# Row maxima of the first attention head computed among the z projections

## The reference

```
qkv    = xn @ qkvw + qkvb                     # 32 heads of 32 features
scores = q k^T / sqrt(32); probs = softmax(scores); ctx = probs v
attn   = ctx @ ow + ob
gate   = softmax over the top 16 of 64 router scores (0 elsewhere)
z      = xn @ A_w^T                            # 64 experts x rank 8 = 512 columns
ffn    = (z * gate) @ B_w^T * 2
out    = x + attn + ffn
```

## Time and profile before

| | us |
|---|---|
| median of 3 runs | 2616.61 |
| profiled execution | 2617.83 |
| its span, first to last instruction | 2615.8 |
| TensorE (PE) busy | 2553.2 |
| GpSimd (POOL) busy | 1603.8 |
| VectorE (DVE) busy | 1511.7 |
| ScalarE (ACT) busy | 1216.7 |

### The profile page before, as it was taken

The page is one execution under the profiler, slowest core; times in us unless marked ns, Lnnn a source line. Parts: engine busy times, 40 slices in busy tenths (PEclk is TensorE's granted clock), DMA queues, the critical chain, the costliest instruction groups (busy, mean ns, idle before and its releaser), DMA issues. The chain is left out here.

```text
span 2615.8 us, 34875 instructions
## 1 busy us (share of the span) xinstructions
PE 2553.2 (98%) x13032; PEld 1655.5 (63%) x13032; DVE 1511.7 (58%) x2522; ACT 1216.7 (47%) x2299; POOL 1603.8 (61%) x529
## 2 busy tenths in 40 slices
PE   7999999999989999999999999999999999969999
PEld 6788888777745555555555555555555555428887
DVE  8511111111188888887888887888878888522231
ACT  2211111111006666666666666666666666650000
POOL 0110011110009999999999999999999999942111
PEclk9999999999959999999999999999999999989999
DMA  4233334121256778778787787787787787523332
GB/s 153 89 121 120 120 117 133 56 72 64 87 143 123 152 159 167 148 162 166 146 166 158 154 166 152 155 170 151 157 169 150 159 167 152 120 97 107 112 113 95
DMA packets 168168, 351.01 MB, mean 134 GB/s; under 512 B 89632, under 2 KB 114720, under 8 KB 137376
## 3 DMA queue, kind: packets, MB, share of 16 engines
q0 software_dynamic: 22320, 162.54, 32.2%
q1 hardware_dynamic: 145712, 186.70, 25.0%
HBM read 122.44 MB, written 63.69 MB: 71 GB/s over the span
## 5 line engine op out<-in xcount | busy, mean ns | idle before, releaser
L921 DVE TENSOR_REDUCE part_max<-ps_b 128x1 f32<-128x512 f32 x2048 | 1252.6, 681 | 276.1 <-PE ps_b L800 276.0
L747 POOL TENSOR_TENSOR psum_p<-psum_p,probs 128x2048 f32<-128x2048 f32 x254 | 1183.6, 4660 | 51.5 <-ACT probs L907 40.1
L907 ACT ACTIVATE probs<-ps_b 128x512 f32<-128x512 f32 x1924 | 971.7, 623 | 350.1 <-PE ps_b L789 348.0
L800 PE MATMUL ps_b<-kp,qp 96*128 96x512 f32 x2048 | 831.4, 413 | 14.5 <-DMA qp<-qk_scr 14.3
L789 PE MATMUL ps_b<-qp,kp 97*128 97x512 f32 x2048 | 840.1, 413 | 5.2 <-ACT probs L907 5.1
L789 PEld LDWEIGHTS ps_b<-qp,kp 97*128 97x128 f32 x2048 | 384.7, 189 | 348.1 <-issue 208.2
L816 PE MATMUL ps_b<-probs,vh 128*32 128x512 f32 x3848 | 468.4, 600 | 0.0
L800 PEld LDWEIGHTS ps_b<-kp,qp 96*128 96x128 f32 x2048 | 397.5, 194 | 101.4 <-DVE part_max L921 38.7
L236 POOL TENSOR_TENSOR wlo<-wraw,whi 128x1024 fp32r<-128x1024 f32 x29 | 69.4, 2395 | 613.2 <-ACT whi L339 613.2
L265 PE MATMUL ps_a<-xhi,whi 128*128 128x512 f32 (+1 forms) x928 | 370.7, 399 | 1.1 <-DVE elo L428 0.9
L265 PE MATMUL ps_a<-xlo,whi 128*128 128x512 f32 (+1 forms) x928 | 367.6, 396 | 0.0
(11 more groups left out here) (79 smaller groups left out, 1159.8 us busy)
## 6 DMA issues: line engine op xcount, KB each, us to landing
psum_q<-probs POOLq DMA_DIRECT2D x155, 1024.0 KB, 7.7
kp<-qk_scr SPq DMA_DIRECT2D x96, 256.0 KB, 4.1
qp<-qk_scr SPq DMA_DIRECT2D x96, 256.0 KB, 7.9
qk_scr<-ehi SPq DMA_DIRECT2D x16, 1024.0 KB, 3.9
qk_scr<-elo SPq DMA_DIRECT2D x16, 1024.0 KB, 6.7
wraw<-wcat SPq DMA_DIRECT2D x29, 512.5 KB, 7.5
craw<-cz_scr SPq DMA_DIRECT2D x16, 768.0 KB, 5.0
stage<-x SPq DMA_DIRECT2D x16, 512.0 KB, 3.8
```

Source lines behind the costliest of these rows:

```text
L747: pool.tensor_tensor(acc[:, :], first[:, :], tile(h, t)[:, :], ALU.add).then_inc(pool_done, 1)
L800: pe.matmul(ps[:, ring_bank(u), :], qp[s][0:PACK, tn * P:(tn + 1) * P], kp[s][0:PACK, b * NQ:(b + 1) * NQ], start=True, stop=True).then_in ...
L907: act.activation(tile(h, t)[:, b * NQ:(b + 1) * NQ], ps[:, n % ST_BANKS, :], ACT.Exp, scale=SCALE).then_inc(exp_done, 1)
L921: dve.tensor_reduce(part_max[hn % 2][:, tn, b:b + 1], ps[:, ring_bank(u), :], AX_X, ALU.max) \
```

## The change

- The space of `ehi` is allocated outside the stages and shared with a new tile `qk0`, which holds `qp` and `kp` of slot 0. `part_max0` too lives through both stages.
- **In stage a**, once all v transposes have been read, SyncE loads q and k of head 0 into `qk0` (six DMAs), and GpSimd sets row 96 of its keys to 1. From the third quarter of the z blocks on, five maxima tiles of head 0 are put among the 24 matmuls of each quarter (after k = 0, 2, 3, 5, 6), four in the last but one, none in the last: 64 in all. They use banks 4 to 7 in turn. VectorE reduces them before it reads that quarter's z product. After the last z matmul TensorE transposes the row maxima, VectorE negates them, and SyncE writes them into row 96, behind the last z stores, and waits for that.
- **In stage b** the prelude is gone. Head 0 starts with `scores_t` at once. The 80 maxima that had to be there by the end of head 0 (64 of head 1, 16 of head 2) are laid among its steps: none in step 0, six a step in steps 1 to 5, five a step in steps 6 to 15. From head 1 on, the order is as before. TensorE no longer waits for identity and ones at the start, but at the first transpose and at head 1. SyncE loads k and q of head 1, then v of heads 0 and 1, then k, q and v of head 2, then `w_early`.
- **In stage c** `xt` and `res` lie in the space of `ehi`.

```diff
@@ stage a, SyncE, ahead of the z stores
+            for u in range(2):
+                sp.wait_ge(stored[u], 32 * QK_BLOCKS // 2)
+            sp.wait_ge(vtr_ready, QB * V_BLOCKS)
+            for row, dst in ((0, qp0), (D, kp0)):
+                for r, hl in enumerate((0, 0, 1) if row == 0 else (0, 1, 0)):
+                    sp.dma_start(dst[r * HD:(r + 1) * HD, :].bitcast(F32), qk_scr[hl, row:row + HD, :]) \
+                        .then_inc(kq0_loaded, 16)
@@ stage a, SyncE, behind the z stores
+            sp.wait_ge(neg0_ready, 1)
+            sp.dma_start(qp0[PACK:PACK + 1, :].bitcast(F32), neg_max0[:, :]).then_inc(negmax0_loaded, 16)
+            sp.wait_ge(negmax0_loaded, 16)
@@ stage a, TensorE
+        def maxima0(q):
+            return [divmod(n, QB) for n in range(5 * (q - 2), min(5 * (q - 1), QB * TT))] if q >= 2 else []
+        def bank0(t, b):
+            return 4 + (QB * t + b) % 4
...
-            for b in range(Z_BLOCKS):
-                qk_block(b % 2, Z0 + b)
+            def maximum0(t, b):
+                n = QB * t + b
+                if n == 0:
+                    pe.wait_ge(kq0_loaded, 16 * 6)
+                    pe.wait_ge(lo_done, quarter(Z0 - 1, 3))
+                wait(pe, max0_free, n - 3)
+                pe.matmul(ps[:, bank0(t, b), :], qp0[0:PACK, t * P:(t + 1) * P], kp0[0:PACK, b * NQ:(b + 1) * NQ],
+                          start=True, stop=True).then_inc(max0_ready, 1)
+            for z in range(Z_BLOCKS):
+                blk = Z0 + z
+                pe.wait_ge(wlo_done, blk + 1)
+                for nb in range(QB):
+                    pe.wait_ge(lo_done, quarter(blk - 1, nb))
+                    left0 = maxima0(QB * z + nb)
+                    n = 0
+                    for k in range(KT):
+                        wk, tk = slice(k * P, (k + 1) * P), slice(nb * NQ, (nb + 1) * NQ)
+                        for w, xx in ((whi, xhi), (whi, xlo), (wlo, xhi)):
+                            last = pe.matmul(ps[:, nb, :], w[:, (z + 1) % 2, wk], xx[:, k, tk],
+                                             start=(n == 0), stop=(n == 3 * KT - 1))
+                            n += 1
+                        if left0 and k in (0, 2, 3, 5, 6):
+                            maximum0(*left0.pop(0))
+                    last.then_inc(mm_ready, 1)
+            pe.wait_ge(rowmax0_ready, 1)
+            pe.wait_ge(max0_free, QB * TT)
+            pe.transpose(ps[0:TT, 4, 0:P], row_max0[:, :], ident[:, :]).then_inc(flip0_ready, 1)
@@ stage a, VectorE, in the z blocks
+                    for t, n in maxima0(QB * b + nb):
+                        dve.wait_ge(max0_ready, QB * t + n + 1)
+                        dve.tensor_reduce(part_max0[:, t, n:n + 1], ps[:, bank0(t, n), :], AX_X, ALU.max) \
+                            .then_inc(max0_free, 1)
@@ stage b, the order of the maxima
-        def first_step(h):
-            return 0 if h >= 0 else -LEAD
+        def maxima_at(h, t):
+            if h == 0:
+                first, count = (6 * (t - 1), 6) if t < 6 else (30 + 5 * (t - 6), 5)
+                return [(1 + n // 64, n // QB % TT, n % QB) for n in range(first, first + count)] if t else []
+            hn, tn = (h + 1, t + LEAD) if t + LEAD < TT else (h + 2, t + LEAD - TT)
+            return [(hn, tn, b) for b in range(QB)] if hn < HEADS else []
@@ stage b, SyncE
-            for h in range(SLOTS):
-                load_keys(h)
-                load_queries(h)
-                load_values(h)
+            load_keys(1)
+            load_queries(1)
+            load_values(0)
+            load_values(1)
+            load_keys(2)
+            load_queries(2)
+            load_values(2)
...
-            load_negmax(0)
@@ stage b, TensorE
-            pe.wait_ge(ident_done, 2)
-            pe.wait_ge(ones_done, 1 + SLOTS)
...
             def step(h, t):
+                ahead = maxima_at(h, t)
                 for b in range(QB):
-                    if h >= 0:
-                        scores_t(h, t, b)
-                    if has_maxima(h, t):
-                        scores(h, t, b)
+                    scores_t(h, t, b)
+                    for u in ahead[b:b + 1]:
+                        scores(*u)
+                for u in ahead[QB:]:
+                    scores(*u)
```

More of the change, by code:

```diff
@@ L242, in _ @@
                     split(blk, (u + 1) % 2)
+            pool.wait_ge(wlo_done, BLOCKS)
+            pool.wait_ge(vtr_ready, QB * V_BLOCKS)
+            pool.memset(kp0[PACK:PACK + 1, :].bitcast(F32), 1.0).then_inc(ones0_done, 1)
+            pool.wait_ge(ones0_done, 1)
         @block.tensor
@@ L525, in sem @@
             return ctx.enter_context(nc.semaphore(name))
[L527 to L528 removed]
+        kp = [qk0[:, 1, :]] + [sb(f"kp{s}", [P, T], F32R) for s in range(1, SLOTS)]
+        qp = [qk0[:, 0, :]] + [sb(f"qp{s}", [P, T], F32R) for s in range(1, SLOTS)]
         vh = [sb(f"vh{s}", [P, TT, HD]) for s in range(SLOTS)]
@@ L538, in attend @@
         recip_b = sb("recip_b", [P, NQ])
-        part_max = [sb(f"part_max{s}", [P, TT, QB]) for s in range(2)]
+        part_max = [part_max0, sb("part_max1", [P, TT, QB])]
         row_max = [sb(f"row_max{s}", [P, TT]) for s in range(2)]
@@ L571, in attend, with loads @@
         ctx_stored = [sem("ctx_stored0"), sem("ctx_stored1")]
[L574 to L579, removed]
-        def first_step(h):
-            return 0 if h >= 0 else -LEAD
+        def loads(h):
+            return h // SLOTS + (1 if h % SLOTS else 0)
+        def maxima_at(h, t):
[4 more added lines that the diff above has]
+            return [(hn, tn, b) for b in range(QB)] if hn < HEADS else []
         ring_order = []
-        for h in range(-1, HEADS):
-            for t in range(first_step(h), TT):
-                if has_maxima(h, t):
-                    ring_order += [("max", h, t, b) for b in range(QB)]
+        for h in range(HEADS):
+            for t in range(TT):
+                ring_order += [("max", *u) for u in maxima_at(h, t)]
                 if t == SUMS_AT and h >= 1:
@@ L731, in _ @@
             pool.memset(ones[:, :], 1.0).then_inc(ones_done, 1)
-            for s in range(SLOTS):
-                pool.wait_ge(ones_done, s + 1)
+            for s in range(1, SLOTS):
+                pool.wait_ge(ones_done, s)
                 pool.memset(kp[s][PACK:PACK + 1, :].bitcast(F32), 1.0).then_inc(ones_done, 1)
-            pool.wait_ge(ones_done, SLOTS + 1)
+            pool.wait_ge(ones_done, SLOTS)
             def add(h, t):
@@ L790, in scores_t, with scores @@
                           qp[s][0:PACK + 1, b * NQ:(b + 1) * NQ], start=True, stop=True).then_inc(st_ready, 1)
-            def scores(h, t, b):
-                hn, tn = target(h, t)
+            def scores(hn, tn, b):
                 s = hn % SLOTS
-                u = ("max", h, t, b)
+                u = ("max", hn, tn, b)
                 wait_ring(pe, u)
                 if tn == 0 and b == 0:
-                    pe.wait_ge(kq_loaded[s], 16 * 6 * (hn // SLOTS + 1))
+                    pe.wait_ge(kq_loaded[s], 16 * 6 * loads(hn))
                 pe.matmul(ps[:, ring_bank(u), :], qp[s][0:PACK, tn * P:(tn + 1) * P],
@@ L861, in step @@
                     sums(h - 1)
[L863 to L866, removed]
+            for h in range(HEADS):
+                if h >= 1:
+                    pe.wait_ge(ones_done, SLOTS)
+                    pe.wait_ge(negmax_loaded[h % SLOTS], 16 * loads(h))
+                for t in range(TT):
                     step(h, t)
@@ L941, in row_maxima @@
             def row_maxima(h):
-                dve.wait_ge(mx_free, 64 * (h + 1))
+                dve.wait_ge(mx_free, 64 * h)
                 dve.tensor_reduce(row_max[h % 2][:, :], part_max[h % 2][:, :, :], AX_X, ALU.max) \
                     .then_inc(rowmax_ready, 1)
[L946 to L950, removed]
+            for h in range(HEADS):
+                for t in range(TT):
+                    for u in maxima_at(h, t):
+                        take_max(*u)
                     if t == RECIPROCAL_AT and h >= 1:
                         reciprocal(h - 1)
-                    if target(h, t)[1] == TT - 1 and h < LAST:
+                    if (h + 1, TT - 1, QB - 1) in maxima_at(h, t):
                         row_maxima(h + 1)
@@ L981, in project_output @@
         clo = sb("clo", [P, 2, OUT_KT, P], F32R)
-        xt = sb("xt", [P, 2, D])
+        xt, res = (ehi[:, i, :].rearrange("p (u d) -> p u d", u=2) for i in range(2))
         ob = sb("ob", [P, D])
-        res = sb("res", [P, 2, D])
         ps = ctx.enter_context(nc.psum_tensor("ps_c", [P, 8, NQ], F32))
```

67 lines of the change are left out of this document (42 added, 25 removed).

## The result

| | before | after |
|---|---|---|
| median | 2616.45 us (4 runs, 2615.69 to 2617.17) | 2596.57 us (4 runs, 2594.53 to 2597.29) |
| profiled execution | 2617.83 us | 2596.82 us |
| its span | 2615.8 us | 2595.0 us |

The ratio after to before is 0.9922, 95% interval 0.9907 to 0.9938: 19.9 us faster. The forecast was 24.6 us faster, 2592.0 us; the time lies 4.6 us above it and inside the range of 2586 to 2603.

What follows compares the result with a forecast made beforehand. VectorE and latencies were taken to bound the prelude, TensorE the steady heads. Terms 14.9 + 0.3 + 5.2 + 0.3 + 9.1 + 53.4 + 0.3 = 83.5 us against 108.1 gave 2592.0 us, range 2586 to 2603.

Steps and rivals of the forecast that it cites:

- The bound named: Prelude bound by VectorE reductions and latencies, steady heads by TensorE; the change attacks only the former stretch, 108.1 us before.
- Maxima among the z products: Stage a, z blocks: 64 added matmuls cost TensorE 14.9 us, with nothing extra for changing operand height.
- Rival C: Z blocks: changes of operand height cost 0.1 us each, 12.8 us more, giving 2605 us; chance 0.08.
- Six loads in front: Stage a: head 0's q and k loads land about when TensorE wants them; 0.3 us, bounds 0 and 3.
- End of stage a: Gap after the last z matmul: the negated maxima are written beside the stores; 0.3 us on top of 5.2.
- Start of head 0: Stage b's start: TensorE stands 9.1 us until the loads of head 1 land, as before the change.
- Its cover: Start of stage b: v of head 0, ones, identity, ScalarE's preparation and `w_early` stay hidden; GpSimd starts earlier, not later.
- Steps 1 to 15: Head 0: VectorE's 80 reductions, coupled to TensorE by four banks, plus low clock take 53.4 us; bounds 47.6 and 56.
- The idling at each pair: Head 0: VectorE idles 0.86 us at each of seven pairs of `values`, 6.0 us in all.
- D: Head 0: the ring couples less, TensorE's own 47.6 us for steps 1 to 15, giving 2586 us; chance 0.10.
- Rivals A and B: Head 0's clock swings, +17 us, 2609 us, chance 0.06; or stays low throughout, +35 us, 2627 us, chance 0.04.
- E: Nothing moves, since loads, block start or something else fills the freed time: 2616 us; chance 0.02.

Runs made afterwards that it cites:

- the changed kernel's second profile: The changed kernel timed again without edits, as reference for the follow-up runs: median 2596.38 us; its profiled z blocks last 110.5 us.
- idle matmuls: Changed kernel plus 24 matmuls with unused result ahead of TensorE's wait for the loads of head 1: median 2596.77 us.
- `values` in each step: Changed kernel with head 0's values one tile in each step instead of two in every second step: median 2595.58 us.
- loads-first kernel: Changed kernel with head 0's six q and k loads issued before the last v block's stores and next weight load: median 2593.83 us.

## Why the prediction was right, and where it was off

- **The bound named.** The prelude went, the rest of the heads did not move, and head 0, from its first maximum on, took 54.0 us, against the whole head's 46.4 before, because of VectorE. Right.
- **Maxima among the z products, 14.9 us.** Measured without the stand: 104.4 us to the transpose, against 716.50 + 0.23 - 627.05 = 89.7 to the same point before: 14.7. Rival C is out: operands of 96 and 128 rows alternate at 0.233 us.
- **Six loads in front, 0.3 us of 0 to 3.** This is the step that was mis-sized. The stand was 2.9, the end of the range, and I gave it no clock: behind it the matmuls ran at 1.2 GHz and cost 1.5 more. For a queue that held 1.5 MB of stores and weights I took the 9.1 us of an empty one. Together 4.4 us for 0.3, and 110.5 - 104.4 = 6.1 in the changed kernel's second profile, so this term alone went past its bound of 3.
- **End of stage a.** The write of the negated maxima did go beside the stores: the gap is 5.3 us, before 5.2.
- **Start of head 0.** 9.3 us as carried over. Its cover held: no wait of TensorE for v of head 0 or for the ones is in the trace there. GpSimd began head 0 at 757.83 us, 47.1 before head 1, where 46 were forecast.
- **Steps 1 to 15.** 54.0 for 53.7. The idling at each pair is 0.72, not 0.86, and the early pairs 7.98, not 8.06; the low clock lasted 4.5 us from the first maximum, 750.94 to 755.4, and cost 1.1 by the idle matmuls, not 0.7. Seven pairs at 0.14 less and a clock dearer by 0.4 would give 53.1; the 0.9 us up to the 54.0 seen are not accounted for, and that the sum came out 0.3 off is in part luck. D is out, since VectorE binds.
- **Rivals A and B, the clock.** It did fall to 1.2 GHz twice and rose again: once behind the stand in z, and once in the gap between the stages, where TensorE stood 5.2 us, from where it stayed low to 755.4. From 755.5 to 805 it is 1.00, through all of the full rings; TensorE's waits for a bank there are 0.4 us at most. So the swing that the Trainium skill's "TensorE: Matmul & The Clock Gate" describes under "A second HAM failure mode: psum-queue depth-cycling" did not come in head 0. It is not ruled out for other pauses of this kernel: in head 30, with waits of 0.30 us, the clock dips in some profiled executions and not in others.
- **E** is out: 19.9 us are gained.

## What to carry to other kernels

A load moved into the shadow of other work is priced with what stands in its queue at that place, and a stand inside dense matmuls with the slow clock behind it: here 2.9 us became 4.4, and 3.2 us became 6.1 in another execution. Where two engines are coupled by a few banks, work out the break of one against the banks' content at the other; that gave 6.86 us for a measured 6.79. When such a break is removed, ask what binds next: idle matmuls and `values` in each step bought head 0 1.1 and 0.5 us alone, and 3 to 4 together.

## What the runs showed that I had not expected

The loads of q and k move at a lower rate than the stores, even with nothing ahead of them in the queue. The DMA view of the loads-first kernel from 626 to 646 us, in slices of 0.5 us, has the loads first and the v stores and weights behind them:

```profile
GB/s 0 0 115 311 262 262 229 197 197 229 246 213 246 246 246 147 238 401 401 385 410 434 410 344 123 0 0 0 0 0 0 0 0 0 0 0 0 0 0 33
```

Some 230 GB/s for the loads, which write 32 partitions each, and 400 for the stores and weights behind them, over 128 partitions. That the number of partitions is the cause was not tested.
